# Two state-space scans of a decoder layer: taps of the convolution in pairs of tiles, state work placed ahead of the gate products, residual loads and their norm moved

## What is computed

```python
zxbcdt = x @ in_proj_w.T
z, xBC, dt = jnp.split(zxbcdt, [D_INNER, D_INNER + CONV_DIM], axis=-1)
dt = jax.nn.softplus(dt + dt_bias)
xBC = jax.lax.conv_general_dilated(xBC, conv_w, ...) + conv_b     # 4 taps
xBC = jax.nn.silu(xBC)
xs, Bmat, Cmat = jnp.split(xBC, ...)
def step(h, inp):
    h = h * dA_t[..., None, None] + (dt_t[..., None] * x_t)[..., None] * B_t[:, None, None, :]
    y_t = jnp.einsum('bhpn,bn->bhp', h, C_t)
y = ys.transpose(1, 0, 2, 3) + D_param[None, None, :, None] * xh
y = y * jax.nn.silu(z)
y = y * jax.lax.rsqrt(jnp.mean(y * y, axis=-1, keepdims=True) + 1e-05) * rms_w
return y @ out_proj_w.T
```

## Time and profile before

| | us |
|---|---|
| median of 3 runs | 4564.73 |
| profiled execution, its own time | 4566.2 |
| its span, first to last instruction | 4564.4 |
| PE busy in the span | 4122.0 (90%) |
| DVE busy | 3084.5 (68%) |
| ACT busy | 1653.2 (36%) |
| POOL busy | 1015.9 (22%) |

### The profile page before, as it was taken

The page is one execution under the profiler, slowest core; times in us unless marked ns, Lnnn a source line. Parts: engine busy times, 40 slices in busy tenths (PEclk is TensorE's granted clock), DMA queues, the critical chain, the costliest instruction groups (busy, mean ns, idle before and its releaser), DMA issues. The chain is left out here.

```text
span 4564.4 us, 72370 instructions
## 1 busy us (share of the span) xinstructions
PE 4122.0 (90%) x26456; PEld 3064.2 (67%) x26456; DVE 3084.5 (68%) x6720; ACT 1653.2 (36%) x3487; POOL 1015.9 (22%) x597
## 2 busy tenths in 40 slices
PE   6999999997899989989868888888898799999999
PEld 4767767674666666666546666666576577778777
DVE  5777777864578787787655746657646576666664
ACT  3334334432333333333325626527446321111111
POOL 0333433333144454444510000000000100000000
PEclk8999999998899999999989999999999899999999
DMA  2110111102001101011043143243242210000000
GB/s 104 36 41 24 39 38 41 40 20 96 24 28 47 43 32 50 34 41 43 30 145 115 48 142 105 65 140 93 69 144 67 91 60 28 28 28 31 28 31 19
DMA packets 144916, 265.88 MB, mean 58 GB/s; under 512 B 25140, under 2 KB 31288, under 8 KB 144568
## 3 DMA queue, kind: packets, MB, share of 16 engines
q1 hardware_dynamic: 144568, 261.27, 17.1%
HBM read 164.58 MB, written 88.08 MB: 55 GB/s over the span
## 5 line engine op out<-in xcount | busy, mean ns | idle before, releaser
L1798 DVE TENSOR_REDUCE xa_mn<-xa_s 128x1 f32<-128x896 f32 (+7 forms) x512 | 373.0, 751 | 135.8 <-PE xa_s L1893 134.8
L1713 ACT ACTIVATE xa_src<-xa_s,xa_mn 128x896 f32<-128x896 f32 (+7 forms) x512 | 378.2, 741 | 230.8 <-DVE xa_mn L1798 229.3
L1899 PE MATMUL xa_gen<-xa_ident,xa_src 128*128 128x128 f32 x2304 | 311.4, 279 | 53.1 <-ACT xa_pT L1722 26.1
L73 PE MATMUL ff_wb<-ff_w_hi,ff_st_hi 128*128 128x512 f32 x768 | 322.1, 419 | 10.0 <-DVE ff_parts L2404 10.0
L1660 POOL TENSOR_TENSOR xa_res<-xa_res,xa_bor 128x512 f32<-128x512 f32 x32 | 40.5, 1271 | 1247.9 <-DMA xa_res<-after_mamba_dram 1247.9
L74 PE MATMUL ff_wb<-ff_w_hi,ff_st_lo 128*128 128x512 f32 x768 | 309.1, 403 | 0.0
L75 PE MATMUL ff_wb<-ff_w_lo,ff_st_hi 128*128 128x512 f32 x768 | 308.2, 401 | 0.0
L1899 PEld LDWEIGHTS xa_gen<-xa_ident,xa_src 128*128 128x128 f32 x2304 | 252.3, 143 | 74.7 <-ACT xa_src L1713 59.5
L1241 PE MATMUL mb_ib<-mb_wc,mb_yT 128*128 128x512 f32 x512 | 265.7, 667 | 1.8 <-DVE mb_y L1012 1.0
L2172 POOL TENSOR_TENSOR ff_mixed<-ff_at,ff_rw 128x1024 f32<-128x1024 f32 x32 | 61.0, 1906 | 869.0 <-DVE ff_at L2432 869.0
L1241 PE MATMUL mf_ib<-mf_wc,mf_yT 128*128 128x512 f32 x512 | 249.7, 634 | 1.8 <-DVE mf_y L1012 1.0
(11 more groups left out here) (510 smaller groups left out, 11303.7 us busy)
## 6 DMA issues: line engine op xcount, KB each, us to landing
xa_qa<-xa_q_dram SPq DMA_DIRECT2D x384, 64.0 KB, 2.0
xa_q_dram<-xa_kq SPq DMA_DIRECT2D x32, 512.0 KB, 2.8
xa_k_dram<-xa_kq SPq DMA_DIRECT2D x32, 512.0 KB, 2.8
xa_ka<-xa_k_dram SPq DMA_DIRECT2D x192, 64.0 KB, 2.0
xa_st<-xa_k_dram SPq DMA_DIRECT2D x192, 64.0 KB, 2.0
mf_xg<-in_x_dram SPq DMA_DIRECT2D x16, 512.0 KB, 5.2
turned_dram<-mf_xt_hi SPq DMA_DIRECT2D x16, 512.0 KB, 2.6
turned_dram<-mf_xt_lo SPq DMA_DIRECT2D x16, 512.0 KB, 4.0
```

Of the source, the lines that this page charges most:

```text
L73: nc.tensor.matmul(out, w_hi, x_hi, start=first, stop=False)
L1713: a_.activation(pq[:, hh, 0:w], s1[g, i, hh][:, 0:w], ACT.Exp, scale=-1.0, bias=mn[:, i % 2, hh:hh + 1], accum_out=sums[:, i // QT, i % QT ...
L1798: v_.tensor_reduce(mn[:, i % 2, hh:hh + 1], s1[g, i, hh][:, 0:(i + 1) * P], AX.X, ALU.min).then_inc(mx_ready.sem, 1)
L1899: last = tr(ps[:, n * P:(n + 1) * P], pq[:, hh, j * P:(j + 1) * P], ident[:])
```

## The change

Five edits in `mamba_pass`. (1) The taps of the front half go through tiles (0,1) with all three taps, then (2,3), instead of four tiles per tap; the first pair waits only for its own projection. (2) On DVE, `carry` comes ahead of the silu product of the front half (`product`) and of the gate products (`gate`). ACT's and PE's `mixed` stay where they were. (3) On PE, the first pair of decays is issued ahead of the waits for yT and for the output's bank. (4) SP loads the residual rows ahead of the next group's `load`. (5) ACT's norm of the residual stands between the second and third exponential. The step sizes (`steps`) stay.

```diff
+SETS = ([(0, 2), (2, 4)], [(4, MT)])
+CONV = (TAPS - 1) * (len(SETS[0]) + len(SETS[1]))
+CONV_FRONT = (TAPS - 1) * len(SETS[0])
...
                 if n % 2 and 0 <= (n + 3) // 2 < NGF:
-                    yield "silu", ((n + 3) // 2, 0)
+                    yield "tanh", (n + 3) // 2
                 if -1 <= n < N:
                     yield "mixed", n
                 if 0 <= n < N:
                     yield "carry", n
+                if n % 2 and 0 <= (n + 3) // 2 < NGF:
+                    yield "product", (n + 3) // 2
+                if -1 <= n < N:
+                    yield "gate", n
+                if backward and 0 <= n - 1 < N:
+                    yield "residual", n - 1
                 if n % 2 == 0 and 0 <= n // 2 + 1 < NGF:
                     yield "silu", (n // 2 + 1, 1)
...
+            def residual_rows(c):
+                if c < N - 1:
+                    wait(sp, out_ready, c - 1)
+                    load_residual(c)
...
-                    if c < N - 1:
-                        wait(sp, out_ready, c - 1)
-                        load_residual(c)
-                    if c == N - 2:
...
+                def normed():
...
                 for q in range(NQ):
+                    if backward and n >= 0 and q == 2:
+                        normed()
                     wait(act, d_full, NQ * c + q)
...
             def taps(g, p):
-                a, b = PARTS[p]
-                wait(dve, tap_ready, MP * g + (b + 1) // 2 - 1)
-                wait(dve, xc_ready, MP * g + (b + 1) // 2 - 1)
-                for i, j in enumerate(range(TAPS - 2, -1, -1)):
...
+                n = CONV * g + p * CONV_FRONT
+                for a, b in SETS[p]:
+                    wait(dve, tap_ready, MP * g + (b + 1) // 2 - 1)
+                    wait(dve, xc_ready, MP * g + (b + 1) // 2 - 1)
+                    for j in range(TAPS - 2, -1, -1):
...
+                        last.then_inc(conv_ready.sem, 1)
+                        yield
+                        wait(dve, conv_ready, n)
+                        n += 1
...
+            def front_product(g):
+                silu(g, 0)
+
-            def mixed(n):
+            def gate(n):
                 c = n + 1
...
             def output(n):
                 c = n + 2
-                if n >= 0:
-                    wait(pe, wc_ready, KI - 1)
-                    wait(pe, yT_ready, 2 * n + 1)
-                    ps = ib.open(pe, ("o", n))
                 for k in range(KI):
                     if c < N and k % 4 == 0:
                         decays(c, k // 4)
+                    if n >= 0 and k == 0:
+                        wait(pe, wc_ready, KI - 1)
+                        wait(pe, yT_ready, 2 * n + 1)
+                        ps = ib.open(pe, ("o", n))
```

More of the change, by code:

```diff
@@ L574, in sums, with load_residual @@
                         sp.dma_start(cr[row:row + 2, g % 2, :].bitcast(F32).rearrange("i (h n) -> i h n", h=Q4), src)                            .then_inc(cr_loaded.sem, 16)
+            def load_residual(c):
+                b, rows = rows_of(c)
+                for t, src in zip(residual(c), (part, x_in)):
+                    sp.dma_start(t, src[b, rows, :]).then_inc(res_loaded.sem, 16)
+            def residual_rows(c):
+                if c < N - 1:
+                    wait(sp, out_ready, c - 1)
+                    load_residual(c)
             def output(c):
@@ L579, in output @@
                 b, rows = rows_of(c)
[L580 to L585, removed]
-                    if c < N - 1:
-                        wait(sp, out_ready, c - 1)
-                        load_residual(c)
-                    if c == N - 2:
-                        wait(sp, base_ready, inner(c))
-                        wait(sp, res_loaded, 2 * c + 1)
-                        load_residual(N - 1)
+                if backward and c == N - 2:
+                    wait(sp, base_ready, inner(c))
+                    wait(sp, res_loaded, 2 * c + 1)
+                    load_residual(N - 1)
                 wait(sp, out_ready, c)
                 sp.dma_start((out if backward else part)[b, rows, :], hb[:, c % 2, :]).then_inc(stored[c % 2].sem, 16)
-            run({"load": load, "weights": weights, "params": parameters, "raw": raw, "sums": sums, "xT": turn_in, "output": output})
+            run({"load": load, "weights": weights, "params": parameters, "raw": raw, "sums": sums, "xT": turn_in, "residual": residual_rows, "output": output})
             for s in stored:
@@ L732, in silu @@
                     last.then_inc(dt_ready.sem, 1)
-                wait(act, conv_ready, (TAPS - 1) * (2 * g + p) + TAPS - 2)
+                wait(act, conv_ready, CONV * g + (CONV if p else CONV_FRONT) - 1)
                 wait(act, x_full, 2 * GT * (g - 1 + p) - 1)
@@ L792, in output @@
                 c = n + 2
-                if backward and n >= 0:
+                def normed():
                     b, rows = rows_of(n)
@@ L800, in output @@
                 if c >= N:
+                    if backward:
+                        normed()
                     return
-                r, t = ring(c)
                 for q in range(NQ):
+                    if backward and n >= 0 and q == 2:
+                        normed()
                     wait(act, d_full, NQ * c + q)
@@ L809, in _ @@
             run({"split": split, "consts": consts, "combine": combine, "xT": turn_in, "front": front, "back": channels, "sums": sums, "inputs": inputs,
-                 "turn": turn, "square": square, "silu": silu, "mixed": mixed, "output": output})
+                 "turn": turn, "square": square, "tanh": front_tanh, "silu": silu, "mixed": mixed, "output": output})
         @block.vector
@@ L878, in taps @@
             def taps(g, p):
-                a, b = PARTS[p]
-                wait(dve, tap_ready, MP * g + (b + 1) // 2 - 1)
-                wait(dve, xc_ready, MP * g + (b + 1) // 2 - 1)
-                for i, j in enumerate(range(TAPS - 2, -1, -1)):
[L884 to L892, removed]
+                n = CONV * g + p * CONV_FRONT
[3 more added lines that the diff above has]
+                    for j in range(TAPS - 2, -1, -1):
+                        o = TAPS - 1 - j if backward else j
+                        for m in range(a, b):
+                            last = v_.scalar_tensor_tensor(cv[:, m, :], xc[:, m, o:o + GN], cw[:, m, j:j + 1], cv[:, m, :],
+                                                           ALU.mult, ALU.add)
+                            if m < b - 1:
+                                yield
+                        last.then_inc(conv_ready.sem, 1)
+                        yield
+                        wait(dve, conv_ready, n)
+                        n += 1
             def silu(g, p):
@@ L918, in halo @@
             def halo(g):
-                wait(dve, conv_ready, (TAPS - 1) * 2 * g - 1)
+                wait(dve, conv_ready, CONV * g - 1)
                 edge = xc[:, :, halo0:halo0 + HALO]
@@ L1072, in output @@
                 v_.tensor_scalar(h, h, hmv[:, 0:1], hr[:, 0:1], ALU.subtract, ALU.mult).then_inc(n_ready.sem, 1)
-            run({"split": split, "consts": consts, "norm": norm, "xT": turn_in, "halo": halo, "steps": steps, "front": front, "taps": taps_back, "silu": silu, "mixed": mixed,
+            run({"split": split, "consts": consts, "norm": norm, "xT": turn_in, "halo": halo, "steps": steps, "front": front, "taps": taps_back, "product": front_product, "silu": silu, "gate": gate,
                  "carry": carry, "total": total,
```

1 line of the change is left out of this document (added).

## The result

The changed kernel takes 4509.55 us, the median of 4 runs (4508.27 to 4511.71), against 4562.67 us for the kernel before beside it on the same chip: a ratio of 0.9884 with a 95% interval of 0.9867 to 0.9901, 53 us less. The forecast was 4527, its range 4492 to 4566.

What follows compares the result with a forecast made beforehand. PE was taken as busiest in both scans, with DVE setting the time in odd backward steps. 4566.2 - 48 backward + 11 forward = 4529 for the profiled execution, 1.5 above the median: 4527 us, range 4492 to 4566.

Steps and rivals of the forecast that it cites:

- The releaser of d0: Backward odd steps: PE's waits ahead of d0 (63.6 us in all) are for the output's bank, freed by an inter-chunk product.
- Rival (d): Backward scan: d0's releaser is another (a DMA, yT), so the forward cost stays alone; 4576 us, chance 0.04.
- Backward sum: Backward scan: state ahead of products gains 3.5 us in seven odd steps, more around last chunks; -48, bounds -25 and -71.
- The cover: Even backward steps: DVE's wait of 5.89 us for PE's sums absorbs `total` starting 2.4 us later; costed at nothing.
- rival (a): Backward scan: once stalls shrink, DVE and POOL bound all steps, half the gain is paid back; 4551 us, chance 0.17.
- the sign that was to show it: Even backward steps: DVE no longer waiting for PE's sums would show the forecast wrong.
- Forward, the banks: Forward even steps and first chunks: PE's turns of the input wait for banks that the gates free; +23.4 us.
- Forward, the half clock behind those waits: Forward: half clock behind 14 waits of the turns, at 8/11 x 1.7 us each; +17, bounds 0 and 34.
- Forward, odd steps: Forward odd steps: shorter stalls -10.4 us, last chunks -5.8, half clock gone in eight steps -13.6.
- the taps at nothing: Taps by pairs remove first-tap waits of 2.25 us forward, 0.35 backward; forward slack, backward held by POOL: no gain.
- Residual: ACT waits 65.4 us for the rows, but in even steps DVE reaches the exponentials later; 0 to -7 us, taken as 0.
- Decays: Last-chunk steps: both decays have free banks and run at once, some 1.1 us gained backward; counted in both sums.

Runs made afterwards that it cites:

- The swap: The changed kernel with the gate products ahead of the front half's silu product, behind the carry as before, in both passes: 4501.84 us, ratio 0.9866.
- the kernel that relieves POOL: The changed kernel with POOL's multiplication by D (line 641) left out of the backward pass: 4462.98 us, ratio 0.9782.
- the split kernel: The changed kernel with DVE's old order in the forward pass and the new order in the backward pass: 4488.8 us, ratio 0.9837.
- the best kernel here: The changed kernel with DVE's old order forward, and carry, gates, product backward: 4472.69 us, ratio 0.9804.

## Why the prediction was right or wrong

**The releaser of d0**: right. The waits ahead of d0 went with the state's and the inter-chunk product's new place, and came back ahead of d1 when the order was undone (86.9 us). Rival (d) is out. That PE's waits lay "almost all in one place" left out 19.1 us ahead of d1; with them in the count, the change takes 30 us of waits away and not 64.

**Backward sum**: right in size (-47 for -48), by other pieces and in part by luck. The prediction let 2 to 3 us of stall stay at odd steps and gave 3.5 us a step. In the trace the odd stall of step 5 falls from 5.7 us (5.28 and 0.46) to 0.74 and the half level goes with it, more than 3.5; but a new stall of 2.88 with half level stands in the even steps. A pair of steps gains 3.5, the seven pairs 23.6 for the 24.5 forecast. In the last chunks the whole stall went, as said; but behind them, in the first chunks, the wait ahead of d1 rose from 0.68 to 2.5, and these stretches gave 18.1 for 22.5. The 7.3 us at the start of the pass are a term that the sum doesn't have (it gave 1.5 to steps 1 and 2).

**The cover**: here a step failed. The held product was costed rightly (3.06; `total` 2.2 later after the state, for 2.4) and then at nothing, because "2.4, and 2.4 more if PE's clock recovers, still fit" in the 5.89 of the earlier trace rows. Only DVE's own lateness was set against that slack. `total` also releases POOL; POOL's run came later and fell on the taps, 4.3 us more (10.62 against 6.34), a term the sum doesn't have. From step 12 before to step 6 after, DVE's wait for the sums fell by 4.0 (5.89 to 1.86) and the taps took 4.3: 8.3 us, which is 2.4 over the slack, and d1's wait in the even step rose by 2.2 (0.66 to 2.88). That is rival (a)'s mechanism, which the prediction named and priced at half the backward gain. It came, though DVE still waits 1.86 for PE's sums, so the sign that was to show it ("if DVE no longer waits") was the wrong one: a wait can remain at the head of a step in which DVE is late at the end. The swap (taps 6.76, even stall 1.09) and the kernel that relieves POOL show that this overlap makes the even steps late. That the sum still held is two errors against each other: the odd steps gave more than taken, the even steps took some back.

**Forward, the banks**: right, 14 waits, 24.1 us for 23.4, and 24.7 us of pass in the split kernel.

**Forward, the half clock behind those waits**: wrong, and most of the error of the total (17 of 17.5 us). The term was 14 x 8/11 x 1.7 = +17, by the nearer pattern of two short waits (0.89, 0.66). Behind none of the 14 waits did the clock fall, as behind the single waits of 1.9, the other pattern at hand (3 of 3). But that pattern is no rule either: with order and taps undone, a single wait of 1.60 was followed by half level in 7 of 11 steps. No row at hand could settle this term.

**Forward, odd steps**: right in size, the cause half told. Without the two terms above, the forecast is -10.4 - 5.8 - 13.6 = -29.8, and the trace has -9.1 - 24.1 = -33. The order gives this with the old taps (1131.2 us, 24.1 of them waits for the banks, for 1133.9 before). But the taps by pairs give it alone as well (1099.0), and together they give it once. So the taps at nothing came true beside this order, and for another reason than the one given. "Forward that time is slack, since PE sets it" was the failed step: in the odd steps that have a stall ahead of d0, DVE sets the time, the stall itself says so the earlier trace rows, and so under the old order a wait of 2.25 ahead of DVE's first tap is on the way, worth 28 us with the half level behind it. The share of 96% for the whole stretch hid it. The prediction had all three rows; by them the taps alone would have brought the forward gain without the 24 us of waits.

**Residual**: nothing, as taken. **Decays**: 5 us or less, in the last chunks, as said.

## What to carry to other kernels

When an instruction is delayed into an engine's slack, follow what it releases on other engines before you cost it at nothing: here the delayed `total` pushed POOL onto DVE's taps, and the taps took as much of the slack (4.3 us) as DVE's own lateness (4.0). A stall, however short, names the engine that sets that step; an idle time ahead of it on that engine is then on the way, whatever the busy shares of the stage say. Two edits that relieve the same stall don't add: what one is worth has to be asked with the other in place. And an order that pays in one pass may cost in another whose banks have other users: the best kernel here uses two.

## What the runs showed of the hardware

POOL's instructions hold not only long DVE instructions. In the kernel with the gates ahead of the product, DVE's step sizes on tiles of 128x32 elements meet POOL's lines 638 and 641. DVE, then POOL:

```profile
1384.88 1.89 DVE L964 TENSOR_TENSOR mb_wd<-mb_ea,mb_wb 128x32 f32<-128x32 f32 x1
1386.69 0.47 DVE L904 SCALAR_TENSOR_TENSOR mb_cv<-mb_xc,mb_cw,mb_cv 128x256 f32<-128x256 f32 x1
1387.09 1.89 DVE L967 TENSOR_TENSOR mb_wa<-mb_wd 128x32 f32<-128x32 f32 x1
1389.78 0.18 DVE L974 SCALAR_TENSOR_TENSOR mb_wb<-mb_wb,mb_wa 128x32 f32<-128x32 f32 x1
...
1384.63 2.10 POOL L638 TENSOR_TENSOR mb_xdt<-mb_xtok,mb_dt 128x1024 f32<-128x1024 f32 x1
1386.80 2.13 POOL L641 TENSOR_TENSOR mb_xtok<-mb_xtok,mb_dsk 128x1024 f32<-128x1024 f32 x1
```

Two instructions of about 0.18 us take 1.89 each and end with POOL's. Between the two POOL instructions, one tap gets through. In step 6 of the changed kernel none does: one tap is held beside line 638 and the next beside line 641 (2.12 us each), one beside line 650 (1.30), and the first, between two POOL instructions, takes 0.71. Against 0.48 these four make up the 4.3 us by which the 15 taps grow. So in these rows each POOL instruction holds one DVE instruction, however short, to about its own end, and at most one more passes before the next. The state, with one input from PSUM, took its 0.68 beside POOL's base, and still does in step 5 above. The Trainium skill (SBUF — State Buffer, section "Who interferes with whom") says that a DVE instruction with two SBUF inputs contends with a GpSimd (here POOL) instruction that reads SBUF, and that the shared port pair is an exclusive lock; these rows agree. What one POOL instruction a step was worth for the whole kernel shows only in the kernel that relieves POOL: 47 us.

Of TensorE's clock: in the changed kernel a single wait of 1.75 us at most ahead of the turns was followed by full level (2.4 GHz) 14 times of 14. With the taps alone undone, the same forward waits were followed by half level (1.2 GHz) once in 14 (at 895.41 us). With order and taps undone, a single wait of 1.60 ahead of d1 was followed by half level in seven steps (5.99 us for 4.28 in step 3) and by full level in four. So the length of the stall alone does not decide; why the cases differ stays open.
